# Attention inside a token: score tiles of 4 tokens by 16 heads in place of 8 by 16, as 16 units in place of 32

## The reference

```python
qkv = (x @ qkv_w + qkv_b).reshape(n, t, 3, H, DH)          # H = 16, DH = 18
attn = jnp.einsum('nthd,ntkd->nthk', q * scale, k)         # 16 x 16 scores per token
attn = jax.nn.softmax(attn, axis=-1)
out = jnp.einsum('nthk,ntkd->nthd', attn, v)
x = x + gate_msa * (out.transpose(0, 2, 1, 3).reshape(n, t, d) @ proj_w + proj_b)
x = x + gate_mlp * mlp(modulate(layernorm(x)))             # 288 -> 1152 -> 288, gelu
```

## Time and profile before

| | |
|---|---|
| three runs | 426.48, 426.82 (median), 428.12 us |
| the profiled execution | 426.86 us, span from first to last instruction 425.1 us |
| granted TensorE clock | 1.00 throughout |
| busy: PE, DVE, ACT, POOL | 402.0 (95%), 290.0 (68%), 232.0 (55%), 112.6 us (26%) |
| `maxima` L737, `scores` L829 | 256 matmuls each, 12.7 us busy each |
| `values` L866 | 512 matmul records, 21.7 us busy |
| reductions L1356, exponentials L1115 | 32 of 1220 ns, 32 of 1032 ns |

### The profile page before, as it was taken

One profiled execution on the slowest core, in us unless ns is written; L12 is line 12 of the kernel. 1 busy time (PEld: TensorE's weight loads), 2 busy tenths in 40 slices (PEclk: granted clock), 3 DMA queues, 4 the chain that ended last, 5 costly groups with the idle time before them and its releaser, 6 DMA issues.

```text
span 425.1 us, 11334 instructions
## 1 busy us (share of the span) xinstructions
PE 402.0 (95%) x4579; PEld 262.3 (62%) x4579; DVE 290.0 (68%) x792; ACT 232.0 (55%) x485; POOL 112.6 (26%) x133
## 2 busy tenths in 40 slices
PE   8999999999989999999977888879999999999996
PEld 4665555666556666666645565657755566666675
DVE  2688885677678846667667866666989776646452
ACT  3356434432266988987786686565776351422100
POOL 5039999950009600000000000004520110101040
PEclk9999999999999999999999999999999999999999
DMA  5999000000000000000000000000000000000011
GB/s 163 303 316 269 24 4 3 11 8 0 2 0 2 2 2 3 2 3 3 2 4 3 5 3 5 2 3 2 2 0 2 14 29 14 15 28 15 29 43 42
DMA packets 7926, 14.68 MB, mean 35 GB/s; under 512 B 2555, under 2 KB 6239, under 8 KB 7748
## 3 DMA queue, kind: packets, MB, share of 16 engines
q1 hardware_dynamic: 7874, 13.96, 11.0%
HBM read 11.52 MB, written 2.38 MB: 33 GB/s over the span
## 4 chain that ended last, share of the span: by engine, by line
PE 74%; DVE 12%; ACT 9%; issue 5%; ACTq 0%; DVEq 0%
PE psum L943 13%; PE psum L959 12%; PE psum L509 9%; PE psum L789 7%; PE psum L773 3%; DVE MX L1356 2%; ACT scratch L1054 2%; PE psum L609 2%; PE psum L866 2%; PE psum L691 2%; PE psum L920 2%; PE psum L621 2%; ACT big L1087 2%; PE psum L737 2%; PE psum L714 2%
## 5 line engine op out<-in xcount | busy, mean ns | idle before, releaser
L943 PE MATMUL psum<-scratch,W 128*128 128x512 f16 (+1 forms) x252 | 57.9, 379 | 0.0
L959 PE MATMUL psum<-W,big 128*128 128x288 f16 x432 | 55.1, 286 | 0.0
L498 POOL TENSOR_TENSOR X<-X,big 128x288 f32<-128x288 f32 x16 | 13.0, 825 | 152.8 <-ACT big L1160 152.5
L1185 ACT ACTIVATE big<-psum 128x512 f32<-128x512 f32 x36 | 21.3, 597 | 57.3 <-PE psum L943 52.3
L959 PEld LDWEIGHTS psum<-W,big 128*128 128x128 f16 x432 | 42.2, 98 | 12.9
L789 PE MATMUL psum<-WQ,scratch 128*128 128x288 f16 (+1 forms) x336 | 49.2, 287 | 1.1 <-DVE scratch L1351 1.1
L1356 DVE TENSOR_REDUCE MX<-psum 128x8 f32<-128x1024 f32 x32 | 39.0, 1220 | 10.9 <-PE psum L737 10.5
L509 PE MATMUL psum<-ident 128*32 128x192 f32 (+3 forms) x142 | 42.7, 385 | 0.0
L1115 ACT ACTIVATE big<-psum 128x1024 f32<-128x1024 f32 x32 | 32.9, 1032 | 14.2 <-PE psum L829 13.9
L943 PEld LDWEIGHTS psum<-scratch,W 128*128 128x128 f16 (+1 forms) x252 | 24.7, 98 | 25.6
L1054 ACT ACTIVATE scratch<-psum,MOD 128x512 f32<-128x512 f32 (+3 forms) x48 | 34.3, 772 | 10.3 <-PE psum L714 6.2
(11 more groups left out here) (218 smaller groups left out, 781.2 us busy)
## 6 DMA issues: line engine op xcount, KB each, us to landing
X<-in_x_dram SPq DMA_DIRECT2D x4, 576.0 KB, 15.1
out_dram<-big SPq DMA_DIRECT2D x16, 144.0 KB, 1.7
big<-in_L_cond_W_dram SPq DMA_DIRECT2D x1, 2268.0 KB
big<-in_L_cond_ada_w_dram SPq DMA_DIRECT2D x2, 864.0 KB, 18.4
stage<-in_L_cond_fc_w_dram SPq DMA_DIRECT2D x1, 1296.0 KB, 19.0
big<-in_L_cond_fc_w_dram SPq DMA_DIRECT2D x1, 1152.0 KB
stage<-in_L_cond_qkv_w_dram SPq DMA_DIRECT2D x1, 864.0 KB
big<-in_L_cond_fc_w_dram SPq DMA_DIRECT2D x3, 144.0 KB
```

The costliest lines, as they stand in the source:

```text
L943: mm = pe.matmul(FB[idx % 3], W1[0:r, w_, P * m:P * m + P], HT[0:r, n % 2, a_, :], start=(p_ == 0), stop=(p_ == 6))
L959: mm = pe.matmul(YB[t % 2][:, 0:D], g[:, a_, f, cols], W2[:, w_, f, :], start=(f == 0 and a_ + w_ == 0), stop=(f == NF - 1 and w_ == 1))
L1185: act.activation(G32[:, idx % 2, :], FB[idx % 3], ACT.Gelu, scale=1.0 / (FINE * FINE)).then_inc(gelu_sb, 1)
```

## The change

Score tiles become 64 x 64 (4 tokens by 16 heads). Each tile of 128 columns is now two, e = 0 and 1, and a unit has 8 such pairs g on both row halves c_: 32 matmuls of 64 x 64 with 64 moving columns, for twice the tokens. Tile (c_, e) takes rows 64 c_ of the array and gives partitions 64 e. The unit fills the same 2 x 512 columns of PSUM, so that reduction and exponential keep their size and their number is halved: `UNITS` is 16, a window is two units. `values` now has for every tile a matmul of 64 rows, 32 output columns and 64 moving columns, with e in another bank. `AHEAD` has 8 units, three slots apart; `LATER` has two units in each of steps 0 to 3. Maxima are turned in steps 2 and 4. `scores` alternates between two bank pairs from unit 5 on. The four parts of `v_late` all stand in the even step, `turn_values` and `v_groups` in the odd one. All `values_out` copies are on ACT. The order of heads and tokens on the partitions differs, for which the matrix `pairs` takes the place of `ident` in `turn`; POOL builds it with two more copies.

```diff
+        pairs = sb("pairs", [P, P])
-        UNITS = 16 * B
+        UNITS = 8 * B
+        HALF = P // 2
...
-        AHEAD = {24 + 3 * s_ // 2: s_ for s_ in range(16)}
-        LATER = {st: 1 for st in range(16)}
-        ROWS_LATER, ROWS_BANK = {8: 2, 16: 3}, {8: VB[0], 16: MXB[0]}
-        PAIRED = 18
-        DVE_AT = 17
+        AHEAD = {24 + 3 * s_: s_ for s_ in range(8)}
+        LATER = {st: 2 for st in range(4)}
+        ROWS_LATER, ROWS_BANK = {2: 2, 4: 3}, {2: VB[0], 4: MXB[0]}
+        PAIRED = 4
...
-            return dst[:, P * first:P * (first + 16)].rearrange("p (v h m) -> p h v m", v=16, h=H)[:, 4 * q:4 * q + 4]
+            return dst[:, P * first:P * (first + 16)].rearrange("p (v h m) -> p h v m", v=32, h=H)[:, 4 * q:4 * q + 4]
...
+            for e in range(2):
+                chain(pool.tensor_copy(pairs.rearrange("p (h e m) -> p e h m", h=H, e=2)[:, e],
+                                       ident[:, P // 2 * e:P // 2 * e + P // 2].rearrange("p (h m) -> p h m", h=H)))
             pool.memset(MOD[:, :, :, :], 0.0).then_inc(consts, 1)
...
             def maxima(s_):
-                for g in range(4):
-                    for c_ in range(2):
-                        mm = pe.matmul(MXB[c_][:, P * g:P * g + P], operand(s_, c_, 0, g, MROWS), operand(s_, c_, 1, g, MROWS),
-                                       start=True, stop=True)
+                for g in range(8):
+                    for e in range(2):
+                        for c_ in range(2):
+                            mm = pe.matmul(MXB[c_][HALF * e:HALF * e + HALF, HALF * g:HALF * g + HALF], operand(s_, c_, 0, g, e, MROWS),
+                                           operand(s_, c_, 1, g, e, MROWS), start=True, stop=True)
...
             def values(s_):
+                for q in (2 * q2, 2 * q2 + 1):
+                    for c_ in range(2):
+                        for g in range(4):
+                            for e in range(2):
+                                rows, at, to = slice(HALF * e, HALF * e + HALF), HALF * (4 * (q % 2) + g), HALF * (4 * c_ + q)
+                                mm = pe.matmul(PO[e][32 * g:32 * g + 32, to:to + HALF], VG[rows, w % 2, c_, 4 * q + g, :],
+                                               E[rows, s_ % 2, c_, at:at + HALF], start=True, stop=True)
...
-                if st % 4 < 2 and 4 <= st // 4 + 1 < UNITS // 4:
-                    for q in range(2 * (st % 4), 2 * (st % 4) + 2):
-                        v_late(st // 4 + 1, q)
-                if st >= 4 and st % 4 == 2:
-                    turn_values(st // 4 - 1)
-                if st % 4 == 3 and st // 4 + 1 < UNITS // 4:
-                    v_groups(st // 4 + 1)
+                if st % 2 == 0 and 4 <= st // 2 + 1 < UNITS // 2:
+                    for q in range(4):
+                        v_late(st // 2 + 1, q)
+                if st >= 2 and st % 2 == 1:
+                    turn_values(st // 2 - 1)
+                if st % 2 == 1 and st // 2 + 1 < UNITS // 2:
+                    v_groups(st // 2 + 1)
...
+                if st >= 2 and st % 2 == 0:
+                    values_out(st // 2 - 1)
+                    if st // 2 + 1 == 4:
+                        for q in range(4):
+                            v_late_out(st // 2 + 1, q)
+                if st % 2 == 1 and st // 2 + 1 < UNITS // 2:
+                    v_out(st // 2 + 1)
```

More of the change, by code:

```diff
@@ L145, in build @@
         o += 2 * CH
-        OT = [scratch[:, o + a_ * 5 * CH // 2:o + a_ * 5 * CH // 2 + CH] for a_ in range(2)]
+        OT = scratch[:, o:o + 2 * CH].rearrange("p (a e j) -> p a e j", a=8, e=2)
         HT = scratch[:, o:o + 5 * CH].bitcast(F16).rearrange("p (a s n) -> p a s n", a=2, s=5)
@@ L720, in turn @@
                         if b < 2:
-                            mm = pe.transpose(f[:, cols], stage[:, at:at + P], ident[:, :])
+                            mm = pe.transpose(f[:, cols], stage[:, at:at + P], pairs[:, :])
                         else:
                             for g in range(3):
-                                mm = pe.matmul(f[32 * g:32 * g + 32, cols], stage[:, at:at + 32], ident[:, :], start=True, stop=True)
+                                mm = pe.matmul(f[32 * g:32 * g + 32, cols], stage[:, at:at + 32], pairs[:, :], start=True, stop=True)
                     mm.then_inc(tr_ready, 1)
             def maxima(s_):
-                if s_ % 4 == 0:
-                    pe.wait_ge(col_done, JOB[(s_ // 4, 1, 3)] + 1)
+                if s_ % 2 == 0:
+                    pe.wait_ge(col_done, JOB[(s_ // 2, 1, 3)] + 1)
                 if s_ == 0:
@@ L826, in scores @@
                     pe.wait_ge(mr_ready, 2)
[L827 to L830, removed]
+                for g in range(8):
+                    for e in range(2):
+                        for c_ in range(2):
+                            mm = pe.matmul(SB[s_ % 2 if s_ > PAIRED else 0][c_][HALF * e:HALF * e + HALF, HALF * g:HALF * g + HALF],
+                                           operand(s_, c_, 1, g, e, MROWS + 1), operand(s_, c_, 0, g, e, MROWS + 1),
+                                           start=True, stop=True)
                 mm.then_inc(s_ready, 1)
@@ L856, in values @@
             def values(s_):
-                w, q = divmod(s_, 4)
+                w, q2 = divmod(s_, 2)
                 pe.wait_ge(exp_done, s_ + 1)
-                if q == 0:
+                if q2 == 0:
                     pe.wait_ge(vg_ready, w + 1)
[L862 to L867, removed]
+                    if w:
+                        pe.wait_ge(ot_ready, 2 * w)
+                for q in (2 * q2, 2 * q2 + 1):
+                    for c_ in range(2):
+                        for g in range(4):
+                            for e in range(2):
+                                rows, at, to = slice(HALF * e, HALF * e + HALF), HALF * (4 * (q % 2) + g), HALF * (4 * c_ + q)
+                                mm = pe.matmul(PO[e][32 * g:32 * g + 32, to:to + HALF], VG[rows, w % 2, c_, 4 * q + g, :],
+                                               E[rows, s_ % 2, c_, at:at + HALF], start=True, stop=True)
                 mm.then_inc(pv_ready, 1)
             def turn_values(w):
-                pe.wait_ge(vg_ready, min(w + 2, UNITS // 4))
-                if w == 1:
+                pe.wait_ge(vg_ready, min(w + 2, UNITS // 2))
+                if w == 0:
                     pe.wait_ge(mr_ready, 1)
@@ L1084, in job_out @@
                 if w == 2:
[L1085 removed]
+                    act.copy(columns(VT, 16 * pr, q)[0:R + 2 * DH], src[0:R + 2 * DH, :].rearrange("p (h v m) -> p h v m", h=4, v=32)).then_inc(col_done, 1)
                 else:
[L1087 removed]
+                    act.copy(columns(QKT[pr // 4][:, w, :], 16 * (pr % 4), q), src.rearrange("p (h v m) -> p h v m", h=4, v=32)).then_inc(col_done, 1)
             for t in range(TPC):
@@ L1127, in values_out @@
             def values_out(w):
-                act.wait_ge(pv_ready, 4 * w + 4)
+                act.wait_ge(pv_ready, 2 * w + 2)
                 if w >= 1:
                     act.wait_ge(o_turned, 2 * w)
-                for c_ in range(2):
-                    act.copy(OT[c_], PO[c_]).then_inc(ot_ready, 1)
+                for e in range(2):
+                    act.copy(OT[:, :, e, :], PO[e].rearrange("p (a j) -> p a j", a=8)).then_inc(ot_ready, 1)
             def v_late_out(w, q):
@@ L1464, in _ @@
                     maximum(s_)
[L1465 to L1471, removed]
+                if st % 2 == 0 and 4 < st // 2 + 1 < UNITS // 2:
+                    for q in range(4):
+                        v_late_out(st // 2 + 1, q)
+                if st >= 2 and st % 2 == 1:
+                    normalise(st // 2 - 1)
             dve.wait_ge(o_norm, UNITS // 2)
```

50 lines of the change are left out of this document (19 added, 31 removed).

## The result

The changed kernel takes 432.82 us (median of 430.62, 432.82 and 434.56); before in the same comparison 426.69. The ratio is 1.0137, 95% interval 1.009 to 1.0184: **slower** by 1.4%, about 6 us. The profiled execution took 451.58 us, as its start is some 14 us longer (its matmuls up to 41 us take up to 1.7 times as long as in before), and like every execution over 1.5% above its kernel's fastest it is left out of the medians and ratios. Only lengths within the later stages are compared.

What follows compares the result with a forecast made beforehand. It took PE, with ACT close behind, to bound the projection slots and rings of waits the attention steps. From 426.86 us, minus 3.0 (slots) and 4.8 (attention), came 419.1; it said 419.2 us, range 415.5 to 427.5.

Steps and rivals of the forecast that it cites:

- bank ring: Late attention windows: late v, copies, turned values, normalising, v groups, ACT's copy through banks 2 and 7; 6.7 us a window.
- maxima ring: Attention steps: PE's maxima and DVE's reduction alternate, one turn 1.72 us, said to hold sixteen steps of the kernel before.
- Pace of the f16 matmuls: New 64 x 64 matmuls: four tiles run at once, so a unit of 32 takes 0.35 us for twice the tokens.
- column tiles in turn: Rival: two tiles on the same rows go one behind the other, 0.55 us a unit; 424.2 us, chance 0.2.
- The second: Rival: every matmul at its present pace, 0.90 us a unit of 32; 451 us, slower, chance 0.1.
- the upper end: Units of values: 0.58 us to the next kind expected; dearer rounds of matmuls would add 0.2 us.
- Part 1, slots: Projection slots: eight maxima units fewer on PE, gain 3.0 us, bounds 1 and 4.5 us.
- the rival in which ACT takes the slots over: Projection slots gain next to nothing as freed PE slots wait for ACT; 422 us, chance 0.15.
- Part 2, attention: Attention steps: 59.05 us instead of 63.8, a gain of 4.8 us, with late windows bound by the bank ring.
- my t from `scores(0)`: Forecast timeline of the attention steps in us, counted from the start of `scores(0)`, ending with the last turn at 59.05.
- Clock 1.00: Sign listed for the forecast: PE's granted clock stays at 1.00, full speed.
- Edits costed at nothing: POOL's extra copies, shorter runs of 4 f16 into `columns`, and `pairs` for `ident`: 0 us.

Runs made afterwards that it cites:

- e4: Kernel before with 64 x 64 tiles for the maxima only, 8 units ahead and 8 in the even steps; 421.15 us, ratio 0.9851.
- e6: Kernel before with each matmul of maxima, scores and values cut into two of 64 columns on the same weights; 432.24 us, ratio 1.011.
- e10: Changed kernel without fillers, with half of the values matmuls (e = 1) left out from window 1 on; 437.03 and 439.55 us.
- e1: Changed kernel with unused matmuls filling PE's waits in the attention steps; 430.58 us, ratio 1.0093.
- e7: e1, fillers kept, with half of the values matmuls (e = 1) left out from window 1 on; 428.77 us, ratio 1.0009.
- e8: Kernel before with seven of eight values matmuls of a unit left out from window 1 on; 426.87 us, ratio 0.9995.
- e11: e4 with the last rows of maxima turned in step 15 and PAIRED 15 for 18; 421.08 us, ratio 0.9878.

## Why the prediction was wrong

**What bounds the kernel: half right.** The bank ring was read well: 7.3 us a window after at full clock (284.01 to 291.29), 6.7 predicted. Most of the difference is in the two units of `values` that it holds (286.60 and 290.50), 0.2 us each; from 289.64 to 291.29 PE works without a wait. The window before it, in part at half clock, lasts 8.3 us (275.67 to 284.01). The reading "sixteen steps are held by the maxima ring" was incomplete, as e4 shows.

**Pace of the f16 matmuls: right.** 0.37 us to the next kind for 0.35, ending after 0.45 us. Both rivals that lived on the pace are out: column tiles in turn (0.55 a unit) and 0.90 a unit. The second has its sign, by another mechanism.

**`values`: mis-sized.** 0.78 us to the next kind (283.23 to 284.01) for 0.58; the upper end that I had named was 0.2 more, and that is what it takes. Sixteen units make up to 3 us.

**Part 1, slots: right.** 48.7 - 44.9 = 3.8 us for 3.0, of which 2.5 are work of PE (2.4 forecast). So the rival in which ACT takes the slots over is out.

**Part 2, attention: wrong, and this is the failed step.** I had 59.05 us, it is 76.9. Against my t from `scores(0)` (at 230.67 in the trace): the eighth maxima at 18.2 for 13.2, `v_late(4)` at 35.4 for 24.4, `v_late(7)` at 60.6 for 45.8. The order of the waits was as I wrote it. Two premises failed, neither of which I had named with a price:

- *That PE gets its instructions in time.* I counted columns and starts, not instructions, and `values` went from 16 records to 64 a unit. The stops add up to 5.3 us, before has none, and each stands where PE enters a new block of 256 instructions. e6 shows this by itself: some 5 us at almost full clock, with the columns and waits of before.
- *"Clock 1.00".* I listed it as a sign, and never asked what emptier steps do to it. I halved the exponentials, reductions and waits of PE for them, left the bank ring as it was, and so forecast a loop in which PE waits over 1 us again and again; that the clock would stay was an assumption. It was 44.4 us at half clock in the profile, at 0.2 us each some 8.9 us.

The sum for the profiled attention: 59.05 + 8.9 + 5.3 + 3 = 76.3 for 76.9 measured; that it comes so close is partly luck, as the 0.2 comes from two other kernels. The same sum for e10, with no 3 us as half of `values` is gone, gives 59.05 + 15.5 + 3.0 = 77.5 for 80.0, so it isn't complete. For the other three executions of after, whose clock of 0.956 to 0.96 means some 36 us at half of 431: 419.1 - 0.8 (the slots) + 7.2 + 5.3 + 3 = 433.8, and they took 430.6 to 434.6.

**What stays open.** The two causes act on each other (a stop is idle time for PE, and at half clock late work leaves longer waits), and no run has one of them wholly without the other in the changed kernel: e1 removed 32.6 us of half clock, which at 0.2 us each is 6.5 us, and gained 2.2 in time, with 1.6 us more of stops and fillers whose own cost no run shows. The split in microseconds is thus an estimate; that each is there is shown by e6 and by e7 with e10. What made the clock fall in after, beyond that filling PE's waits takes most of the falls away (44.4 to 11.8 us, 77.5 to 18.5), is open too: e8, with less work on PE but the waits of before, has 6.8 us of them.

**Edits costed at nothing: right.** POOL's copies, the runs of 4 in `columns`, `pairs`: all of them are in e4 and e11, and those are faster than before. ACT's copies of 512 elements (L1087, now L1098) take 596 ns in both kernels.

## What to carry to other kernels

Cutting matmuls into smaller tiles costs instructions even where the array takes them at full pace: count PE's instructions per microsecond in the stage, not its columns alone (256 in 4.4 us and more didn't stop PE in before, 256 in about 4 us or less did in e6), and keep small tiles for the part where they relieve another engine (here the maxima in the slots). Work taken off PE in a stage bound by a ring of waits can cost its clock, and then all of PE's links in the ring get longer; look at the granted clock first when a kernel with less work takes longer. And try the parts of a change apart: one half of this one was worth some 5 us.

## What the hardware showed that was not expected

- 32 matmuls of 64 x 64 on four quadrants end 0.45 us after the first start; with some 0.21 us for one, 31 starts fall into 0.24, one each 8 ns. In the trace the four of a group start 3 to 4 ns apart, and a group follows the one before in some 31 ns (the second in some 50). The Trainium skill ("TensorE: Matmul & The Clock Gate", back-to-back issue gap), whose rule the prediction weighed, has no starts closer than about 25 ns: that agrees with the 31 ns on one tile and doesn't hold across tiles.
- PE stops for 0.2 to 2.2 us in the middle of a burst where small matmuls come fast, each time at the start of a block of 256 of its instructions and 1.2 to 1.6 us after a packet of the instruction queue has ended. In e6 it gets no more than a block each 3.5 to 4.1 us.
- PE at half clock for 78.5 us without a break (e10, 219.1 to 297.6), though it is shown busy for 59.0 of 77.6 us; in the full-clock stretch of after from 280.30 it is busy for 17.82 of 27.30, no larger a share. The busy share of a row doesn't tell which clock a stretch gets, the more so as a slower clock makes it larger.
